# Sampling matrices split first and turned by the DMA engines instead of TensorE, in a fused attention and deformable-convolution kernel

## The chip, the core and the metric

The kernel is one program on one core of a Trainium2 chip. Its instructions run on five engines with a queue each: TensorE (PE, matmuls), VectorE (DVE), ScalarE (ACT), GpSimd (POOL) and SyncE (SP, which here only issues DMAs). Engines wait for each other by semaphores. The metric is the device time of one execution in microseconds, lower is better, as the median over runs.

## The reference

The input is `x`, 32 images of 192 channels and 32 x 32 pixels in float32. Two blocks follow, each behind a group normalization (32 groups) and each added to its input:

```python
x = x + attention(_gn(x))          # attention between channels, 1x1 projections
x = x + deform_block(_gn(x))

# attention, N = 1024 pixels
q, k, v = split(w_qkv @ x)                         # each 192 x N
attn = softmax(einsum('bcn,bdn->bcd', q, k) * 48 ** -0.5)
out = w_out @ (attn @ v) + b_out

# deformable 3x3 convolution
offset = clip(conv(x, off_w, off_b), -8, 8)        # 18 maps
mask = 2 * sigmoid(conv(x, mask_w, mask_b))        # 9 maps
# tap k of pixel (i, j) reads x, bilinearly, at (i - 1 + ky + dy, j - 1 + kx + dx), times the mask
y = einsum('bckhw,ock->bohw', p, proj_w) + proj_b
yn = (y - mean) * rsqrt(var + 1e-5) * gamma + beta # mean and variance over all images
return gelu(yn)
```

## The kernel before

The convolution samples after projecting. For each tap k, `z` is the projection of `x` with that tap's 192 x 192 weights, and the bilinear sampling is a matrix S_k of hat functions: the entry for output pixel p and source pixel (r, c) is mask x hat(y_p - r) x hat(x_p - c). So y = sum over k of S_k z_k. An image is cut into 8 tiles of 128 output pixels (4 rows). For a tile and one of the three rows of taps ky, the near sources are 8 rows of pixels, two chunks of 128. If an offset reaches further, a separate `far_pass` runs at the end of the image; a flag decides, and in this data the near branch is taken.

The names:
- A *step* is a tile and a ky: 24 per image. A *unit* is a step and one of its two source chunks: 48 per image (`UNITS`).
- `ay` and `bx` hold the row and column hats. They are made from `off`, the clipped offsets, by a subtraction (for `bx` on POOL, `column_distance`, line 1328; for `ay` on DVE, line 1122) and two activations on ACT (`column_hats`, lines 853 and 855; lines 844 and 846).
- `sT` is S transposed, output pixels on the partitions, 3 taps x 256 source pixels in float32. POOL makes one per step (line 1346), in a ring of 3.
- TensorE turns it (`turn_s`, line 653): three float32 transposes of 128 x 128 per unit, into one of two PSUM banks `sps`.
- Each turned unit is split in two float16 parts, high and rest: ACT casts to `sh` (line 896), DVE subtracts to `sl` (line 1157); a ring of 3.
- `convolve` multiplies (lines 670 to 672): three taps x (sh zh, sh zl, sl zh), nine matmuls of 192 columns into `acc`. After six units a tile is full; ACT copies it to `ypm`, TensorE turns it to `yt`, and DVE scales it to `ych` (`scale_y`, line 1219).
- `z` is made by `z_group` (lines 639 to 643), five matmuls of 288 columns per unit into one of two PSUM banks `zps`, ten units ahead (`AHEAD`), and split likewise by ACT (line 862) and DVE (line 1151). `z_group` of a unit waits for the `z` split of two units before.

The order is written out by hand. For each image `part1` walks over the 48 units on each engine, and `part0(u, b + 1, ...)`, the whole attention block, second normalization and offset convolution of the next image, is cut into 48 numbered pieces that are put behind the unit of the same number. Pieces that the prediction speaks of, by number: 0 to 4 statistics of the input; 6 to 10 first normalization on ACT and its residues on DVE (line 1014); 12 to 22 attention; 23 to 26 the sum `x1` and its statistics; 30 to 33 second normalization on ACT; 32 to 36 its residues and the moves of its planes to shifted copies on DVE (lines 1014 and 1020 to 1024); 38 and 39 the offset convolution on PE; 40 `off` (line 1118); 41 to 46 the hats. The DMAs on SyncE are few: `attended` stores `x1` and loads the input of the image after the next, `convolved` stores `y`. Batch statistics need all images, so a last pass reads `y` and `x1` again, applies the GELU and stores the output (from about 3805 us on).

## Time and profile before

| | |
|---|---|
| median of 3 runs | 4033.15 us (4030.4 to 4049.43) |
| the profiled execution | 4041.7 us, its span 4039.9 us, mean granted TensorE clock 0.966 |
| busy, share of the span | PE 88%, DVE 66%, ACT 52%, POOL 35% |
| DMA | 170.89 MB in all, mean 42 GB/s |

Time is busy time by the profiler; matmuls overlap in the record, so that a busy PE is not PE at its peak. A wait is idle time of an engine just before an instruction, named by what released it.

### The profile page before, as it was taken

To read this page: it belongs to the slowest core of one execution; us is meant where nothing else is said; L and a number is where in the kernel's file an instruction comes from. 1 tells how busy PE (TensorE), PEld (TensorE's weight loads), DVE (VectorE), ACT (ScalarE), POOL (GpSimd) and SP (SyncE) were. 2 spreads that over 40 slices of the span, in tenths; PEclk is the share of its full clock that TensorE was granted. 3 is DMA by queue.
4 is the path that set the end of the run, shared out by engine and by line. 5 is a ranking of instruction groups with operands and counts; after the bars stand their busy time and mean duration, and the time that the engine had idled before them with its cause. 6 is when DMAs were issued, how large, how long until landed. Compare 5 with 4: busy or idle time off the path is not lost.

```text
span 4039.9 us, 109164 instructions
## 1 busy us (share of the span) xinstructions
PE 3554.5 (88%) x38338; PEld 3036.9 (75%) x38338; DVE 2650.4 (66%) x5834; ACT 2108.1 (52%) x4790; POOL 1412.7 (35%) x1165
## 2 busy tenths in 40 slices
PE   3999999999999999999999999999999999999600
PEld 2788878888887878888887878788788888877600
DVE  3666776676777666666776676677666766776522
ACT  1555555555555555555555555555555555554422
POOL 1333333333333333434333333333333433333311
PEclk8999999999999999999999999999999999999855
DMA  2000000000000000000010000000000000000398
GB/s 63 20 11 28 28 28 20 28 28 28 10 28 28 20 28 28 28 17 21 29 28 21 28 28 28 10 28 28 28 20 28 28 24 14 28 28 10 96 370 299
DMA packets 50796, 170.89 MB, mean 42 GB/s; under 512 B 9664, under 2 KB 10880, under 8 KB 50176
## 3 DMA queue, kind: packets, MB, share of 16 engines
q1 hardware_dynamic: 39584, 136.75, 11.2%
q0 software_dynamic: 7168, 25.17, 1.6%
q8 instruction: 365, 5.98, 0.6%
q14 instruction: 255, 2.09, 0.2%
q10 hardware_dynamic: 3424, 0.90, 0.1%
HBM read 87.29 MB, written 75.50 MB: 40 GB/s over the span
## 4 chain that ended last, share of the span: by engine, by line
PE 65%; DVE 13%; issue 9%; DMA 4%; POOL 4%; ACT 3%; DVEq 1%; SPq 1%; ACTq 0%; POOLq 0%
PE sps L653 10%; PE acc L672 6%; PE acc L670 6%; PE acc L671 6%; PE l L581 4%; PE zps L639 3%; PE zps L643 3%; PE zps L641 3%; PE zps L640 3%; PE zps L642 3%; DVE zl L1151 3%; POOL sT L1346 3%; DMA xn<-x_scratch 2%; DVE sl L1157 2%; PE l L513 2%
## 5 line engine op out<-in xcount | busy, mean ns | idle before, releaser
L1346 POOL TENSOR_TENSOR sT<-ay,bx 128x768 f32<-128x768 f32 x768 | 1149.3, 1507 | 1394.6 <-PE sps L653 1326.2
L1157 DVE TENSOR_TENSOR sl<-sps,sh 128x384 f16<-128x384 f32 x1536 | 847.8, 552 | 560.7 <-ACT sh L896 555.9
L672 PE MATMUL acc<-zh,sl 128*128 128x192 f16 x4608 | 1134.6, 246 | 22.4 <-issue 22.4
L670 PE MATMUL acc<-zh,sh 128*128 128x192 f16 x4608 | 1134.6, 246 | 0.3 <-ACT ypm L923 0.3
L671 PE MATMUL acc<-zl,sh 128*128 128x192 f16 x4608 | 1134.5, 246 | 0.0
L896 ACT CAST sh<-sps 128x384 f16<-128x384 f32 x1536 | 741.4, 483 | 705.3 <-PE sps L653 696.9
L862 ACT CAST zh<-zps 128x288 f16<-128x288 f32 x1536 | 620.2, 404 | 668.4 <-PE zps L643 643.7
L1151 DVE TENSOR_TENSOR zl<-zps,zh 128x288 f16<-128x288 f32 x1536 | 694.2, 452 | 353.5 <-ACT zh L862 345.2
L653 PE MATMUL sps<-eye,sT 128*128 128x128 f32 x4608 | 786.3, 280 | 130.7 <-DVE sl L1157 96.6
L653 PEld LDWEIGHTS sps<-eye,sT 128*128 128x128 f32 x4608 | 531.7, 141 | 287.0 <-DVE sl L1157 158.0
L672 PEld LDWEIGHTS acc<-zh,sl 128*128 128x128 f16 x4608 | 451.3, 98 | 25.4 <-issue 25.3
L671 PEld LDWEIGHTS acc<-zl,sh 128*128 128x128 f16 x4608 | 451.3, 98 | 17.2
L670 PEld LDWEIGHTS acc<-zh,sh 128*128 128x128 f16 x4608 | 451.1, 98 | 2.5 <-DVE sl L1157 0.5
L639 PE MATMUL zps<-wpr_h,x_hi_a 128*128 128x288 f16 x1344 | 385.0, 286 | 0.8 <-DVE zl L1151 0.3
L640 PE MATMUL zps<-wpr_l,x_hi_a 128*128 128x288 f16 x1344 | 384.9, 286 | 0.0
L642 PE MATMUL zps<-wpr_h,x_hilo_b 128*128 128x288 f16 x1344 | 384.9, 286 | 0.0
L643 PE MATMUL zps<-wpr_l,x_hilo_b 128*128 128x288 f16 x1344 | 384.9, 286 | 0.0
L641 PE MATMUL zps<-wpr_h,x_lo_a 128*128 128x288 f16 x1344 | 384.9, 286 | 0.0
L1328 POOL TENSOR_TENSOR bx<-off,cx_sb 128x576 f32<-128x576 f32 x128 | 155.6, 1216 | 459.2 <-DVE off L1118 459.2
L1310 POOL TENSOR_TENSOR rstd<-gvar,mhalf 128x2 f32<-128x2 f32 x64 | 44.9, 702 | 557.7 <-DVE gvar L1008 557.7
L581 PE MATMUL l<-wof,x2s_hi_a 128*128 128x54 f16 x1536 | 183.0, 186 | 9.8 <-DVE x2w_hilo_b L1024 9.8
L581 PE MATMUL l<-wof,x2s_lo_a 128*128 128x54 f16 x1536 | 182.8, 186 | 0.0
(200 smaller groups left out, 6488.8 us busy)
## 6 DMA issues: line engine op xcount, KB each, us to landing
xin<-in_x SPq DMA_DIRECT2D x32, 512.0 KB, 5.2
xin<-in_x SPq DMA_DIRECT2D x64, 256.0 KB, 5.7
x_scratch<-x SPq DMA_DIRECT2D x32, 512.0 KB, 2.8
y_scratch<-ych SPq DMA_DIRECT2D x32, 512.0 KB, 2.7
zh<-y_scratch SPq DMA_DIRECT2D x20, 512.0 KB, 11.6
zl<-x_scratch SPq DMA_DIRECT2D x20, 512.0 KB, 12.8
out<-zh POOLq DMA_DIRECT2D x20, 512.0 KB, 9.3
x_scratch<-x SPq DMA_DIRECT2D x32, 256.0 KB, 3.5
```

What stands on the lines that cost most here:

```text
L581: mm = pe.matmul(o, src[:, row * W:(row + ROWS_T) * W], wof[:, m, k].rearrange("p i j -> p (i j)"), start=(k == 0 and n == 0), stop=(k == ...
L639: pe.matmul(o, at(0), wpr_h[:, 0, ky, n], start=True, stop=False)
L640: pe.matmul(o, at(0), wpr_l[:, 0, ky, n], start=False, stop=False)
L653: mm = pe.transpose(sps[u % 2][:, kx * P:(kx + 1) * P], sT[:, g, kx, c * P:(c + 1) * P], eye32[:, :])
L670: pe.matmul(acc[:, 0:C], s_h, zh[:, j, ky, z], start=start and kx == 0, stop=False)
L671: pe.matmul(acc[:, 0:C], s_h, zl[:, j, ky, z], start=False, stop=False)
L672: mm = pe.matmul(acc[:, 0:C], s_l, zh[:, j, ky, z], start=False, stop=stop and kx == 2)
L862: act.copy(z_piece(zh, g, par), zps[:, g % 2, 0:KO // 2]).then_inc(z_hi, 1)
L896: act.copy(sh[:, u % S_RING].rearrange("p k n -> p (k n)"), sps[u % 2][:, 0:3 * P]).then_inc(s_hi, 1)
L1151: dve.tensor_tensor(z_piece(zl, g, par), zps[:, g % 2, 0:KO // 2], z_piece(zh, g, par), ALU.subtract)\
L1157: dve.tensor_tensor(one(sl), sps[u % 2][:, 0:3 * P], one(sh), ALU.subtract).then_inc(s_lo, 1)
L1346: pool.tensor_tensor(sT[:, p % ST_RING].rearrange("p k (r x) -> p k r x", r=R), a, x_, ALU.mult)\
```

## The change

`sT` stays as POOL makes it, but it is split before it is turned. Per step, ACT casts all 768 columns of `sT` to the high half of `sT_hl`, and DVE subtracts for the low half; both now read SBUF. SyncE then issues one transposing DMA (`dma_start_transpose`) that turns the twelve 128 x 128 blocks (high and low, three taps, two chunks) into `s_hl`, a ring of 4 slots with a completion semaphore each, and `convolve` waits for the slot instead of for `s_lo`. The splits run four steps ahead (`S_AHEAD`), and the next image's preparation is moved up by six units (`EARLY`), so that its last six pieces' places are taken by the first six of the image after. Since the hats are needed sooner than the old ones are free, `bx` becomes a ring of two quarter-images, and its later quarters are made at other places. The far pass gets tiles of its own.

```diff
-        bx = sb("bx", [P, 2, TILES * TAPS, W])
+        BX_RING = 2
+        bx = sb("bx", [P, BX_RING, 2 * TAPS, W])
...
-        S_RING = 3
-        sh = sb("sh", [P, S_RING, 3, P], F16)
-        sl = sb("sl", [P, S_RING, 3, P], F16)
+        S_RING = 4
+        sT_hl = sb("sT_hl", [P, S_RING, 2, 3 * R * W], F16)
+        s_hl = sb("s_hl", [P, S_RING, 2, 3, 2, P], F16)
+        f_sh = sb("f_sh", [P, 3, P], F16)
+        f_sl = sb("f_sl", [P, 3, P], F16)
...
-            part1(0, 0, True, FRONT)
+            part1(0, 0, 2, FRONT)
...
+        def prepare(part0, u, b, par, more):
+
+            if u + EARLY < UNITS:
+                if more:
+                    part0(u + EARLY, b + 1, 1 - par)
+            elif more == 2:
+                part0(u + EARLY - UNITS, b + 2, par)
+
+        def prepare_second(part0):
+            for u in range(EARLY):
+                part0(u, 1, 1)
...
+        STEPS = 3 * TILES
+        S_AHEAD = 4
+        EARLY = 6
+
+        def s_step(u):
+
+            if u >= UNITS - S_AHEAD:
+                return u - (UNITS - S_AHEAD), True
+            if u % 2 == 0 and u // 2 + S_AHEAD < STEPS:
+                return u // 2 + S_AHEAD, False
+            return None, False
+
+        def turned(p, b):
+
+            return 16 * (STEPS // S_RING) * b + 16 * (p // S_RING) + 16
...
+            def turn_s(p, b):
+                if p >= S_RING or not first(b):
+                    sp.wait_ge(sz_done, UNITS * b + 2 * (p - S_RING) + 2)
+                    sp.sem_inc(turn_free, 1)
+                sp.wait_ge(s_lo, STEPS * b + p + 1)
+                sp.sem_inc(turn_begun, 1)
+                slot = p % S_RING
+                sp.dma_start_transpose(s_hl[:, slot].rearrange("p h k c n -> p (h k c) n"),
+                                       sT_hl[:, slot].rearrange("p h n -> p (h n)")).then_inc(s_turned[slot], 16)
+
+            def image(b, more, edge=None):
+                for p in range(STEPS):
+                    turn_s(p, b)
+                    if p == 8 and not first(b):
+                        convolved(b - 1)
...
+                    if p == 15 and more:
+                        attended(b + 1, more == 2)
...
-            def turn_s(u, b):
-                t, ky, c = u // 6, u % 6 // 2, u % 2
-                if c == 0:
-                    pe.wait_ge(st_made, 24 * b + 3 * t + ky + 1)
-                if u >= 2 or not first(b):
-                    pe.wait_ge(s_lo, UNITS * b + u - 1)
-                g = (3 * t + ky) % ST_RING
-                for kx in range(3):
-                    mm = pe.transpose(sps[u % 2][:, kx * P:(kx + 1) * P], sT[:, g, kx, c * P:(c + 1) * P], eye32[:, :])
-                mm.then_inc(s_ps, 1)
-
             def convolve(u, b, par):
                 i, ky, c = u // 6, u % 6 // 2, u % 2
-                pe.wait_ge(s_lo, UNITS * b + u + 1)
+                if c == 0:
+                    pe.wait_ge(s_turned[u // 2 % S_RING], turned(u // 2, b))
...
-                    if more:
-                        part0(u, b + 1, 1 - par)
+                    prepare(part0, u, b, par, more)
...
-            def split_s(u, b):
-                act.wait_ge(s_ps, UNITS * b + u + 1)
-                if u >= S_RING or not first(b):
-                    act.wait_ge(sz_done, UNITS * b + u - S_RING + 1)
-                act.copy(sh[:, u % S_RING].rearrange("p k n -> p (k n)"), sps[u % 2][:, 0:3 * P]).then_inc(s_hi, 1)
+            def split_s(p, b):
+                act.wait_ge(st_made, STEPS * b + p + 1)
+                if p >= S_RING or not first(b):
+                    act.wait_ge(s_turned[p % S_RING], turned(p - S_RING, b))
+                act.copy(sT_hl[:, p % S_RING, 0], sT[:, p % ST_RING].rearrange("p k n -> p (k n)")).then_inc(s_hi, 1)
...
-                    if u % 12 == 4 and u < 36:
-                        column_hats(u // 12 + 1, b, par)
+                    if u in (3, 13, 25):
+                        column_hats((3, 13, 25).index(u) + 1, b)
...
-            def split_s(u, b):
-                dve.wait_ge(s_hi, UNITS * b + u + 1)
-                one = lambda t: t[:, u % S_RING].rearrange("p k n -> p (k n)")
-                dve.tensor_tensor(one(sl), sps[u % 2][:, 0:3 * P], one(sh), ALU.subtract).then_inc(s_lo, 1)
+            def split_s(p, b):
+                dve.wait_ge(s_hi, STEPS * b + p + 1)
+                dve.tensor_tensor(sT_hl[:, p % S_RING, 1], sT[:, p % ST_RING].rearrange("p k n -> p (k n)"),
+                                  sT_hl[:, p % S_RING, 0], ALU.subtract).then_inc(s_lo, 1)
...
+                if q >= BX_RING or not first(b):
+                    pool.wait_ge(st_made, STEPS * b + 6 * (q - BX_RING) + 6)
...
                     if p >= ST_RING or not first(b):
-                        pool.wait_ge(s_ps, UNITS * b + 2 * (p - ST_RING) + 2)
+                        pool.wait_ge(s_lo, STEPS * b + p - ST_RING + 1)
...
-                    if p in (1, 4, 10):
-                        column_distance((1, 4, 10).index(p) + 1, b, par)
+                    if p in (1, 6, 12):
+                        column_distance((1, 6, 12).index(p) + 1, b, par)
                     if more:
-
-                        for u in (2 * p - 4, 2 * p - 3):
-                            part0(u, b + 1, 1 - par)
+                        for u in range(2):
+                            part0(2 * (p - S_AHEAD) + EARLY + u, b + 1, 1 - par)
```

The order on VectorE around the moves, before (in the first image; `sl` and `zl` are the two splits, `x_hilo_b` a residue, `x2s` and `x2w` the shifted planes and seams):

```order
L1151 TENSOR_TENSOR zl<-zps,zh 128x288
L1014 TENSOR_TENSOR x_lo_a<-xn,x_hi_a 128x1024
L1157 TENSOR_TENSOR sl<-sps,sh 128x384
L1151 TENSOR_TENSOR zl<-zps,zh 128x288
L1020 COPY x2s_hi_a<-x_hi_a 128x32x31
L1021 COPY x2s_hi_a<-x_hi_a 128x32x31
L1023 COPY x2w_hi_a<-x_hi_a 128x96
L1024 COPY x2w_hi_a<-x_hi_a 128x96
L1157 TENSOR_TENSOR sl<-sps,sh 128x384
L1151 TENSOR_TENSOR zl<-zps,zh 128x288
L1014 TENSOR_TENSOR x_hilo_b<-xn,x_hilo_b 64x1024
L1157 TENSOR_TENSOR sl<-sps,sh 128x384
```

The same place after (`sT_hl` is the new split of `sT`):

```order
L1185 TENSOR_TENSOR zl<-zps,zh 128x288
L1048 TENSOR_TENSOR x_lo_a<-xn,x_hi_a 128x1024
L1185 TENSOR_TENSOR zl<-zps,zh 128x288
L1054 COPY x2s_hi_a<-x_hi_a 128x32x31
L1055 COPY x2s_hi_a<-x_hi_a 128x32x31
L1057 COPY x2w_hi_a<-x_hi_a 128x96
L1058 COPY x2w_hi_a<-x_hi_a 128x96
L1190 TENSOR_TENSOR sT_hl<-sT,sT_hl 128x768
L1185 TENSOR_TENSOR zl<-zps,zh 128x288
L1048 TENSOR_TENSOR x_hilo_b<-xn,x_hilo_b 64x1024
L1185 TENSOR_TENSOR zl<-zps,zh 128x288
L1054 COPY x2s_lo_a<-x_lo_a 128x32x31
```

What moved: every preparation piece is still followed by one `zl` split, but the `sl` split of each unit has become one wider split of `sT` in every second unit.

The order on GpSimd at the turn from one image to the next, before; the row of line 1328 is the next image's first column distance, which waits for `off`:

```order
L1346 TENSOR_TENSOR sT<-ay,bx 128x768
L1326 REGISTER_ALU
L1328 TENSOR_TENSOR bx<-off,cx_sb 128x576
L1342 ISA
L1346 TENSOR_TENSOR sT<-ay,bx 128x768
L1338 ISA
L1340 ISA
L1342 ISA
L1346 TENSOR_TENSOR sT<-ay,bx 128x768
```

After (line 1373 is the column distance, 1392 makes `sT`, the three ISA rows in a run carry waits for the hats):

```order
L1392 TENSOR_TENSOR sT<-ay,bx 128x768
L1369 REGISTER_ALU
L1371 ISA
L1373 TENSOR_TENSOR bx<-off,cx_sb 128x576
L1387 ISA
L1392 TENSOR_TENSOR sT<-ay,bx 128x768
L1387 ISA
L1392 TENSOR_TENSOR sT<-ay,bx 128x768
L1383 ISA
L1385 ISA
L1387 ISA
L1392 TENSOR_TENSOR sT<-ay,bx 128x768
```

What moved: the column distance stands one `sT` tile earlier; two tiles of the old image follow it where one did, and then the waits and the new image's first tile.

The order on SyncE in the loop, before: the stores of `y` and `x1` follow each other directly.

```order
L415 ISA
L415 DMA xin<-in_x 64x1024
L434 ISA
L434 DMA y_scratch<-ych 128x1024
L435 ISA
L435 DMA y_scratch<-ych 64x1024
L426 ISA
L427 ISA
L427 DMA x_scratch<-x 128x1024
L428 ISA
```

After, around the ninth step of an image:

```order
L475 DMA_TRANSPOSE s_hl<-sT_hl 128x12x128
L470 ISA
L472 ISA
L475 DMA_TRANSPOSE s_hl<-sT_hl 128x12x128
L470 ISA
L472 ISA
L475 DMA_TRANSPOSE s_hl<-sT_hl 128x12x128
L465 ISA
L465 DMA y_scratch<-ych 128x1024
L466 ISA
L466 DMA y_scratch<-ych 64x1024
L470 ISA
```

What moved: each store of `y` now stands in a row of 24 transposing DMAs per image, each behind a wait for a free slot (line 472's ISA row) and one for the split.

## Rows read from the trace of the kernel before

**Rows 1.** The page: busy time and share by engine, and the chain that ended last.

```profile
PE 3554.5 (88%) x38338; PEld 3036.9 (75%) x38338; DVE 2650.4 (66%) x5834; ACT 2108.1 (52%) x4790; POOL 1412.7 (35%) x1165
...
PE 65%; DVE 13%; issue 9%; DMA 4%; POOL 4%; ACT 3%; DVEq 1%; SPq 1%; ACTq 0%; POOLq 0%
PE sps L653 10%; PE acc L672 6%; PE acc L670 6%; PE acc L671 6%; PE l L581 4%; PE zps L639 3%; PE zps L643 3%; PE zps L641 3%; PE zps L640 3%; PE zps L642 3%; DVE zl L1151 3%; POOL sT L1346 3%; DMA xn<-x_scratch 2%; DVE sl L1157 2%; PE l L513 2%
```

**Rows 2.** Windows: from:to, length, each engine's busy time, granted clock, DMA.

```profile
1512.80:1522.90 10.10, 9.32 (x92) 8.18 (x90) 9.35 (x21) 4.84 (x14) 4.46 (x4) 1.00 0.02 6
1522.90:1532.90 10.00, 9.98 (x96) 9.08 (x95) 7.51 (x21) 7.71 (x17) 6.01 (x7) 1.00 0.19 66
...
1590.60:1597.70 7.10, 6.97 (x72) 6.25 (x70) 6.05 (x13) 7.10 (x13) 4.01 (x4) 1.00 0.01 3
1597.70:1606.00 8.30, 5.85 (x53) 4.44 (x50) 8.24 (x18) 3.13 (x9) 2.87 (x2) 1.00 0.00 0
...
1615.30:1628.30 13.00, 12.28 (x122) 10.84 (x120) 9.67 (x26) 8.95 (x24) 7.97 (x6) 1.00 0.01 1
sum 115.50, PE 110.61 PEld 94.54 DVE 80.54 ACT 63.86 POOL 42.56; mean PE 11.06 PEld 9.45 DVE 8.05 ACT 6.39 POOL 4.26
```

**Rows 3.** The chain in a plain stretch: start, length, what.

```profile
1516.95 0.33 PE sps L653 x3
...
1518.02 0.12 PE zps L639
...
1518.63 0.33 PE sps L653 x3
```

**Rows 4.** Line 1118, the clipped offsets: durations, first and last start.

```profile
L1118 DVE TENSOR_SCALAR off<-off x32: 234/235/236, 104.8 to 3713.3; 128x144 f32<-128x144 f32 x32
```

**Rows 5.** Groups by line: shapes, count | busy us, mean ns | idle before.

```profile
L1157 DVE TENSOR_TENSOR sl<-sps,sh 128x384 f16<-128x384 f32 x1536 | 847.8, 552 | 560.7 <-ACT sh L896 555.9 <-issue 1.2
...
L896 ACT CAST sh<-sps 128x384 f16<-128x384 f32 x1536 | 741.4, 483 | 705.3 <-PE sps L653 696.9 <-PE acc L672 2.5
L1151 DVE TENSOR_TENSOR zl<-zps,zh 128x288 f16<-128x288 f32 x1536 | 694.2, 452 | 353.5 <-ACT zh L862 345.2
L862 ACT CAST zh<-zps 128x288 f16<-128x288 f32 x1536 | 620.2, 404 | 668.4 <-PE zps L643 643.7
...
L810 ACT COPY xt<-l 128x768 f16<-128x768 f16 x128 | 102.1, 799 | 13.8 <-PE l L525 13.8
```

**Rows 6.** Three lines: duration ns min/median/max, first and last start.

```profile
L1014 DVE TENSOR_TENSOR xl_a<-xn,xh_a x32: 1226/1710/1716, 46.3 to 3628.5; 128x1024 f16<-128x1024 f32 x32
...
L1023 DVE COPY x2w_hi_a<-x_hi_a x32: 175/1448/1451, 92.5 to 3692.8; 128x96 f16<-128x96 f16 x32
...
L1346 POOL TENSOR_TENSOR sT<-ay,bx x768: 1470/1482/1698, 108.2 to 3797.5; 128x768 f32<-128x768 f32 x192
```

**Rows 7.** Groups by line, ACT alone: normalization and hats.

```profile
L853 ACT ACTIVATE bx<-bx 128x576 f32<-128x576 f32 x128 | 88.5, 691 | 0.1
...
L795 ACT ACTIVATE xn<-x,nbias,rstd 128x1024 f32<-128x1024 f32 x64 | 80.5, 1258 | 14.0 <-POOL nbias L1314 14.0
```

**Rows 8.** Timeline at an image's turn: start, length, engine, line [idle before <-releaser].

```profile
1502.79 1.16 POOL L1328 TENSOR_TENSOR bx<-off,cx_sb 128x576 f32<-128x576 f32 x1 [14.28 <-DVE off L1118]
...
1506.27 0.31 PEld L653 LDWEIGHTS sps<-eye,sT 128*128 128x128 f32 x3 [0.92 <-DVE sl L1157]
```

**Rows 9.** DMA queues, and issues with KB each and median us to landing.

```profile
q1 hardware_dynamic: 39584, 136.75, 11.2%
...
q10 hardware_dynamic: 3424, 0.90, 0.1%
...
xin<-in_x SPq DMA_DIRECT2D x64, 256.0 KB, 5.7
x_scratch<-x SPq DMA_DIRECT2D x32, 512.0 KB, 2.8
```

**Rows 10.** SyncE's time for one issue: ns min/median/max.

```profile
L427 SPq DMA_DIRECT2D x_scratch<-x x32: 337/346/373, 83.3 to 3677.6; - x32
```

More of the change, by code:

```diff
@@ L218, in build @@
         st_made = sem("st_made")
-        s_ps = sem("s_ps")
+        s_turned = [sem(f"s_turned{i}") for i in range(S_RING)]
+        turn_free = sem("turn_free")
+        turn_begun = sem("turn_begun")
         s_hi = sem("s_hi")
@@ L312, in pairs_of_images @@
         @contextmanager
-        def pairs_of_images(eng, start, end):
+        def pairs_of_images(eng, start, end, step=2):
             name, only = f"images_{nc.next_id()}", [eng.engine]
@@ L320, in pairs_of_images @@
                 edge = []
-                yield nc.snap(count, min_val=start, max_val=end - 1), edge
-                nc.regs_alu(count, count, 2, op=ALU.add)
+                yield nc.snap(count, min_val=start, max_val=end - step), edge
+                nc.regs_alu(count, count, step, op=ALU.add)
                 eng.br_lt(count, end, on_true=f"{name}_loop", on_false=f"{name}_end").branch_hint(edge[0])
@@ L901, in part1 @@
                         split_z(g, b, par)
-                    split_s(0, b)
-                    split_s(1, b)
+                    for p in range(S_AHEAD):
+                        split_s(p, b)
+                    prepare_second(part0)
                 for u in units:
@@ L906, in part1 @@
                         edge.append(act.mark_branch_hint_location())
[L907 to L910 removed]
+                    p, of_next = s_step(u)
+                    if p is not None and not of_next:
+                        split_s(p, b)
+                    elif p is not None and more:
+                        split_s(p, b + 1)
                     if u == 24:
@@ L1236, in part1 @@
                         split_z(g, b, par)
-                    split_s(0, b)
-                    split_s(1, b)
+                    for p in range(S_AHEAD):
+                        split_s(p, b)
+                    prepare_second(part0)
                 for u in units:
```

108 lines of the change are left out of this document (53 added, 55 removed).

## The prediction

> **What bounds the kernel now.** First the page's busy shares and the chain that ended last [rows 1]: TensorE is busy 88% of 4039.9 us and holds 65% of the chain, with the transposes of `sT` (line 653) its largest line, 10%. Then one image of the steady loop cut into stretches [rows 2]; the reader should compare the columns stretch by stretch, since a share over the span hides what each stretch waits for. From 1597.7 us VectorE (DVE) is busy 8.24 of 8.30 us and TensorE (PE) only 5.85; from 1512.8 DVE has 9.35 of 10.10; over all ten stretches, 115.5 us, PE has 110.6, DVE 80.5, ScalarE (ACT) 63.9, GpSimd (POOL) 42.6. The granted clock is 1.00, the 2.4 GHz level. Then the chain inside a plain stretch [rows 3]: a unit (one of 48 per image) takes 1.68 us, from 1516.95 to 1518.63, of which the three transposes are 0.33, the nine products of lines 670 to 672 0.74 and the five `zps` products 0.61. So PE sets the pace, except where VectorE is full.
>
> Line 1118 runs once per image, at 104.8 us first and 3713.3 last [rows 4]: the mean image is 3608.5 / 31 = 116.4 us, and the one of rows 2 stands for all. My sums are against the profiled run, 4041.7 us. The median, 4033.15, is 8.5 lower; I subtract that at the end.
>
> **Removed from PE.** 4608 transposes, three per unit, 0.33 us per unit: 48 x 0.33 = 15.8 us per image, 507 us for 32, if PE set the pace everywhere. Image: 115.5 - 15.8 = 99.7. A plain unit would be 1.68 - 0.33 = 1.35 us, and a step (two units, one `sT` tile) 2.70.
>
> **Changed on ACT and DVE.** Per step ACT casts 2 x 483 ns and DVE subtracts 2 x 552 ns from PSUM, beside two `z` splits at 404 and 452 [rows 5]. Afterwards each has one operation of 768 columns from SBUF. For ACT the copy of line 810 has that width: 799 ns. For DVE, 288 columns at 452 and 384 at 552 give 1.04 ns a column, so 768 is 952 ns [rows 5]. ACT saves 0.17 and DVE 0.15 us a step, which leaves 80.5 - 3.7 = 76.8 us of DVE work per image, 77% of 99.7. What DVE costs is decided by where that work lies.
>
> **Given back where DVE is full.** The next image's preparation keeps its operations and moves up six units; the work on `y` stays. PE may run ahead of the `z` splits by two buffers: one unit and the nine products, 1.35 + 0.74, less cast and subtraction, 0.40 + 0.45, leave some 1.2 us; then PE stands.
> (a) Lines 1014 and 1020 to 1024, preparation units 32 to 36, now at 26 to 30. Today 15.4 us go by from 1590.6 to 1606.0 for seven units of 1.68, so 3.6 us of stall. Afterwards DVE needs in units 26 to 31: six `z` and half `s` splits at 0.92, 5.5; the residues 1.71 and, at the line's least, 1.22; moves of 2.46 + 2.46 + 1.2, whose largest part is a 96-column copy of 1.45 [rows 6]; `scale_y`, 1.07. Together 15.6 us. Units 24 and 25 add 1.8, and ACT holds DVE up there: two normalizations at 1.26, two hat operations at 0.69, two casts of `z` and one of `s` are 5.5 us [rows 5, 7], of whose 3.7 beyond DVE's own I count half. 1.8 + 1.9 + 15.6 - 1.2 = 18.1 us for eight units, where PE alone needs 10.8: 7.3 of stall against 3.6 now. Lost: 3.7 us per image.
> (b) Preparation units 41 to 47 and the next image's units 0 to 9. Three stretches of rows 2 (from 1615.3, 1512.8 and 1522.9) hold these 17 units in 33.1 us with DVE busy 26.5. Without transposes PE needs 27.5, and DVE 26.5 - 1.2 = 25.3, 92% of it, in pieces of up to 1.7 us, with the splits of steps 0 to 3 packed one per unit at 44 to 47. Two engines that wait for each other at such a load don't both fit: I take 12% of 27.5, 3.3 us.
>
> **Moved on POOL.** The column distance of the next image stood before step 23 and now stands before step 22. Today POOL runs it as soon as `off` is clipped, for 1.16 us, `sT` follows, and PE loses 0.92 us to the split behind it at 1506.27 [rows 8]. Afterwards `off` comes in unit 34, and ACT wants step 22 at unit 36, with its `z` cast queued behind that wait; PE feels it at unit 38. `off` 1.1 + distance 1.2 + `sT` 1.5 + cast 0.8 + subtraction 0.95 + a `z` split 0.45, 6.0 us, against the 4.5 to 6 us until unit 38's `z`: between 0 and 3 us with the lag of DVE, I take 1.5.
>
> **Added: 768 transposing DMAs**, each 128 x 1536 half floats, 393 KB, on SyncE's queue. This trace has none. Lower bound: queue q1 moves 136.75 MB in 11.2% of the 16 engines' 4039.9 us, 302 GB/s, so 1.3 us. The nearest row is q10's, whose 3424 packets have 263 bytes in the mean and took 0.1% of that time, 19 ns each; the transfer has 1536 source pieces of 256 bytes, 96 per engine: 1.8 us. Upper bound: if every 32-byte piece of the destination cost those 19 ns, 768 per engine are 14.6 us [rows 9]. I take 1.8, and for latency the stores of 512 KB, landed 2.8 us after issue, and 0.35 us of SyncE's time per issue [rows 9, 10]: some 3.5 us. The rate stands under the 2.70 of a step. The slot is free one step after its split begins, which leaves three steps, 8.1 us, even beside an input load of 5.7 us [rows 9]. So PE's work hides it, and if it takes longer than a step this cover is gone (rivals 1 and 4). Only step 0 of an image is tight, split at unit 44 and used at 48: 0.8 + 0.95 + 1.2 of lag + 3.5 = 6.5 against four units and the last `y` transposes, 5.8, and the statistics product: I put 0.3 us. Behind SyncE's new waits stand its stores and loads; their data is there by units 6 and 20, and they are issued behind steps 8 and 15, at units 10 and 24: nothing.
> By the Trainium skill (Advanced Engine Details and Errata, X-Bar Transpose (TRN2)) a transposing DMA reaches 350 to 400 GB/s; DMA: Bandwidth & Descriptors (Latency and other measured facts) has 261 with a non-contiguous middle dimension. By these it would be 1.0 to 1.5 us, an estimate that no run here shows yet.
>
> **The sum.** Per image 99.7 + 3.7 + 3.3 + 1.5 + 0.3 = 108.5, 7.0 less than 115.5. 31 x 7.0 = 217; the last image has no preparation and gains about 12; the start grows by about 5 (four steps and six preparation units ahead of the loop). 4041.7 - 224 = 3818, in terms of the median 3809. **Forecast 3810 us**, own range 3700 to 3920 (gains of 3.5 to 10.5 us per image).
>
> **Rivals.**
> 1. *The transposing DMA is too slow*, and SyncE's queue sets the pace. It decides from 115.5 / 24 = 4.8 us per step; 1.8 and 14.6 lie on both sides. At 5.5 us an image is 132 and the run 4033 + 32 x 16.5 = 4560; at 14.6 it would pass 11000. For it: no row shows a transpose, and the destination comes in 32-byte runs. Against: the source pieces have 256 bytes. 16%.
> 2. *DVE and POOL block each other.* The new subtraction reads two SBUF tensors, the old one PSUM and SBUF. Line 1014, with two SBUF inputs, takes at least 1226 ns but 1710 in the median, and the 96-column copy 175 against 1448, close to one POOL operation (1482) more [rows 6]. If each of 768 subtractions lost 0.48 us, 369, half of them where DVE is full, 185: 3995. At 1.27 each, 4300. Against: POOL's next `sT` is released by this subtraction itself and is over 1.5 us later, while the next subtraction comes at least 1.75 later. 12%, three quarters of it still faster.
> The Trainium skill (SBUF — State Buffer, SBUF: two separate sides) has this as an exclusive lock, held for the whole instruction by either a GpSimd operation or a DVE one with two SBUF inputs. Rows 6 agree.
> 3. *Nothing is given back*: 4033 - 507 = 3526, up to 3620 with part of (a). Against it stands DVE's 8.24 of 8.30 us [rows 2]. 8%.
> 4. *Transposes at 3.3 to 4.6 us*: at 3.9 some six plain steps an image lose 1.2 us each, less the slack 3 to 5: 3810 + 32 x 4 = 3940. 5%, two fifths of it no change.
>
> **Chances.** Forecast 59%, rivals 16, 12, 8, 5. Faster by over 0.5% (what a measurement of this kernel can tell from no change): 59 + 9 + 8 + 3 = 79%. Within 0.5%: 2 + 2 = 4%. Slower: 16 + 1 = 17%. The range 3580 to 4040 leaves out rival 1 and half of rival 3.
>
> **What would show it.** Right: transposes landing in under 5 us, PE idle for `z` splits only and mostly beside line 1014 and the copies, plain units of 1.35 us, images of 105 to 112 us, a subtraction of about 0.95 us. Wrong: PE waiting for a transposed slot throughout the image (rivals 1, 4), a subtraction of over 1.3 us in the median (rival 2), or units of 1.35 us even beside the moves (rival 3).

## The result and the profile after

| | before | after |
|---|---|---|
| median | 4032.94 us (4030.4 to 4049.43, 4 runs) | **4277.0 us** (4273.95 to 4278.61, 4 runs) |
| ratio, 95% interval | | **1.0595 [1.0566, 1.0624]**, slower |
| span of the profiled run | 4039.9 us | 4276.9 us |
| granted TensorE clock, mean | 0.966 | 0.897 |

The page of the kernel after, where it answers to [rows 1] and [rows 9]; the last two rows are two of its DMA rows.

```profile
PE 3346.2 (78%) x33730; PEld 2667.4 (62%) x33730; DVE 2659.5 (62%) x5066; ACT 2010.7 (47%) x4022; POOL 1517.8 (35%) x1165
...
PEclk8899989999999999899899998899998999999855
...
q1 hardware_dynamic: 1243808, 438.83, 54.2%
...
s_hl<-sT_hl SPq DMA_TRANSPOSE x768, 3.7
```

TensorE has less to do and is busy a smaller share of a longer run. The clock row has 8s all through the loop; the kernel before has 9s there. (The chain of waits covers only 8% of this run's span, so I read waits and windows instead.) The first and last start of the clipped offsets, against [rows 4]:

```profile
L1152 DVE TENSOR_SCALAR off<-off x32: 234/234/236, 106.0 to 3946.9; 128x144 f32<-128x144 f32 x32
```

(3946.9 - 106.0) / 31 = 123.9 us per image, where it was 116.4 and 108.5 was forecast. Two windows of about one image (columns as in [rows 2]):

```profile
1604.00:1616.00 12.00, 7.65 (x58) 5.66 (x57) 8.77 (x20) 4.04 (x10) 6.14 (x6) 0.91 0.82 119
...
1672.00:1696.00 24.00, 18.10 (x154) 14.63 (x152) 16.78 (x32) 14.09 (x26) 9.84 (x9) 0.93 0.75 160
```

TensorE is busy 64 and 75% in them, VectorE 73 and 70%. And the clock is under 1.00, which no window of [rows 2] was. Such long windows hide what each wait looks like, so here are shorter ones of the same image around four of TensorE's waits: units 5, 15, 28 to 32, and 38:

```profile
1622.40:1626.40 4.00, 1.68 (x16) 1.07 (x13) 1.55 (x3) 3.63 (x8) 3.11 (x3) 1.00 0.53 98
1649.10:1655.00 5.90, 3.54 (x25) 2.15 (x23) 3.74 (x7) 1.03 (x3) 2.59 (x2) 0.99 0.58 108
1684.10:1700.20 16.10, 10.57 (x181) 8.57 (x179) 15.00 (x27) 8.01 (x15) 4.59 (x4) 1.00 0.72 120
1709.90:1715.60 5.70, 2.92 (x20) 2.26 (x19) 3.68 (x9) 4.36 (x9) 3.57 (x3) 0.77 0.24 45
```

They differ. In the third, around the moves, VectorE is busy 15.00 of 16.10 us; in the first ScalarE is, 3.63 of 4.00; in the second and fourth no engine is near full. TensorE's waits, in all, times, longest, after:

```profile
PE zps L688 <- DVE zl L1185: 332.6, 312, 5.4
PE l L553 <- DVE mv L1032: 95.4, 64, 14.2
PE l L561 <- DVE gram L1105: 75.7, 32, 2.8
PE acc L710 <- ACT ypm L958: 55.8, 39, 1.7
...
PE acc L710 <- DMA s_hl<-sT_hl: 0.6, 1, 0.6
```

and before:

```profile
PE sps L653 <- DVE sl L1157: 96.6, 125, 1.2
...
PE l L512 <- DVE gram L1071: 21.5, 32, 2.8
...
PE l L504 <- DVE mv L998: 16.9, 2, 14.2
```

The transposing DMAs are waited for once, 0.6 us. What TensorE waits for is VectorE's `z` split, the statistics and the Gram matrix. What such a wait leaves behind shows around the Gram matrix, in windows of 2 us and in the timeline:

```profile
1647.00:1649.00 2.00, 2.00 (x22) 1.83 (x21) 0.46 (x1) 1.49 (x6) 2.00 (x3) 1.00 0.38 71
...
1651.00:1653.00 2.00, 0.03 (x1) 0.03 (x1) 1.92 (x7) 0.05 (x1) 1.48 (x1) 1.00 0.37 70
1653.00:1655.00 2.00, 2.00 (x9) 0.99 (x10) 0.29 (x1) 0.00 (x0) 0.00 (x0) 0.98 0.69 127
1655.00:1657.00 2.00, 2.00 (x13) 1.74 (x13) 0.65 (x1) 1.26 (x3) 0.00 (x0) 0.50 0.00 0
1657.00:1659.00 2.00, 2.00 (x9) 1.16 (x8) 0.77 (x2) 0.40 (x1) 1.48 (x1) 0.67 0.00 0
```

```profile
1611.98 0.25 PE L712 MATMUL acc<-zh,s_hl 128*128 128x192 f16 x1
1612.06 0.25 PE L710 MATMUL acc<-zh,s_hl 128*128 128x192 f16 x1
...
1652.97 0.59 PE L561 MATMUL l<-wo,gram 128*128 128x192 f32 x2 [2.36 <-DVE gram L1105]
...
1655.25 0.37 PE L712 MATMUL acc<-zh,s_hl 128*128 128x192 f16 x1
1655.41 0.37 PE L710 MATMUL acc<-zh,s_hl 128*128 128x192 f16 x1
```

TensorE stands 2.36 us, works on, and then has the granted clock 0.50, the 1.2 GHz level: the same matmuls start 0.16 us apart instead of 0.08. A wait can be paid a second time, in slow columns behind it.

**Where the time went.** A mean clock c over a span is 2 x (1 - c) of it at half rate: 2 x 0.103 x 4276.9 = 881 us after, 2 x 0.034 x 4039.9 = 275 before. 606 us more, which cost half of that, 303 us. The spans differ by 237 = -507 (transposes removed) + 303 (clock) + 441, and this rest is what TensorE waits more. By its matmul records, as a mean of images 2 to 29:

| per image, us | period | no matmul under way | at 1.2 GHz |
|---|---|---|---|
| before | 116.3 | 5.6 | 0.1 |
| after | 124.2 | 19.5 | 19.9 |

116.3 - 15.8 + (19.5 - 5.6) + (19.9 - 0.1) / 2 = 124.3. Below, *gaps* and *half clock* are the two last columns. The rule that time at the low clock costs half of itself is also in the Trainium skill (TensorE: Matmul & The Clock Gate, Terms); this sum agrees with it.

### The profile page after: what moved, and what is told of

It is laid out like the page before. It is cut to its first block and busy times, and to the rows that moved or that the text cites. A ratio compares the mean times of both kernels' runs of the same rounds, so it can differ in the third digit from the quotient of the medians.

```text
span 4276.9 us, 97266 instructions
## 1 busy us (share of the span) xinstructions
PE 3346.2 (78%) x33730; PEld 2667.4 (62%) x33730; DVE 2659.5 (62%) x5066; ACT 2010.7 (47%) x4022; POOL 1517.8 (35%) x1165
## 5 line engine op out<-in xcount | busy, mean ns | idle before, releaser
L1392 POOL TENSOR_TENSOR sT<-ay,bx 128x768 f32<-128x768 f32 x768 | 1235.2, 1622 | 1304.0 <-ACT bx L888 685.8
L1190 DVE TENSOR_TENSOR sT_hl<-sT,sT_hl 128x768 f16<-128x768 f32 x768 | 877.2, 1142 | 656.8 <-ACT sT_hl L929 656.1
L710 PE MATMUL acc<-zh,s_hl 128*128 128x192 f16 x4608 | 1190.3, 258 | 84.5 <-ACT ypm L958 55.8
L711 PE MATMUL acc<-zl,s_hl 128*128 128x192 f16 x4608 | 1189.1, 258 | 27.3 <-issue 27.3
L712 PE MATMUL acc<-zh,s_hl 128*128 128x192 f16 x4608 | 1188.7, 258 | 0.0
L929 ACT CAST sT_hl<-sT 128x768 f16<-128x768 f32 x768 | 638.8, 832 | 264.7 <-POOL sT L1392 167.3
L688 PE MATMUL zps<-wpr_h,x_hi_a 128*128 128x288 f16 x1344 | 410.3, 305 | 287.2 <-DVE zl L1185 284.5
L710 PEld LDWEIGHTS acc<-zh,s_hl 128*128 128x128 f16 x4608 | 471.7, 102 | 210.0 <-issue 89.4
L711 PEld LDWEIGHTS acc<-zl,s_hl 128*128 128x128 f16 x4608 | 472.8, 103 | 73.0 <-issue 29.9
L712 PEld LDWEIGHTS acc<-zh,s_hl 128*128 128x128 f16 x4608 | 474.9, 103 | 6.4 <-issue 1.3
L688 PEld LDWEIGHTS zps<-wpr_h,x_hi_a 128*128 128x128 f16 x1344 | 137.1, 102 | 364.3 <-DVE zl L1185 356.1
L957 ACT COPY ypm<-acc 128x192 f32<-128x192 f32 x256 | 81.9, 320 | 325.1 <-PE acc L712 324.6
```

Source lines behind the costliest of these rows:

```text
L688: pe.matmul(o, at(0), wpr_h[:, 0, ky, n], start=True, stop=False)
L710: pe.matmul(acc[:, 0:C], s_h, zh[:, j, ky, z], start=start and kx == 0, stop=False)
L711: pe.matmul(acc[:, 0:C], s_h, zl[:, j, ky, z], start=False, stop=False)
L712: mm = pe.matmul(acc[:, 0:C], s_l, zh[:, j, ky, z], start=False, stop=stop and kx == 2)
L929: act.copy(sT_hl[:, p % S_RING, 0], sT[:, p % ST_RING].rearrange("p k n -> p (k n)")).then_inc(s_hi, 1)
L1190: dve.tensor_tensor(sT_hl[:, p % S_RING, 1], sT[:, p % ST_RING].rearrange("p k n -> p (k n)"), sT_hl[:, p % S_RING, 0], ALU.subtract).then ...
```

## The experiments

All times stand against the kernel before on the same chip, 4028 to 4034 us. Each run has the gaps and half clock of one image.

| run | median us | ratio to before, 95% | gaps | half clock |
|---|---|---|---|---|
| e1 hats early | 4107.75 | 1.0188 [1.0155, 1.022] | 17.1 | 13.2 |
| e2 distance later | 4251.4 | 1.0563 [1.0517, 1.0609] | 21.1 | 13.3 |
| e3 no transposing DMA | 4212.05 | 1.0438 [1.0401, 1.0476] | 19.4 | 15.8 |
| e4 before, a third of the transposes | 3939.23 | 0.9779 [0.9744, 0.9814] | 10.4 | 4.6 |
| e5 = e1 + e2 | 4090.66 | 1.0146 [1.0109, 1.0184] | 18.0 | 9.7 |
| e6 e1, two units ahead, not six | 4380.45 | 1.0866 [1.0834, 1.0899] | 22.6 | 20.2 |
| e7 after + fillers | 4143.36 | 1.027 [1.0239, 1.0302] | 9.5 | 0.1 |
| e8 e5, `z` split first | 4301.83 | 1.067 [1.063, 1.0709] | 20.4 | 21.6 |
| e9 e5 + fillers | 4045.01 | 1.0023 [1.0009, 1.0037] | 10.7 | 0.6 |
| e10 no moves | 4204.97 | 1.041 [1.0373, 1.0447] | 18.8 | 16.9 |
| e11 four `z` banks | 4332.89 | 1.0752 [1.0717, 1.0786] | 20.6 | 25.9 |
| e12 e5, four `z` banks | 4189.53 | 1.0397 [1.0359, 1.0435] | 18.6 | 19.3 |
| e13 e5, 3 `z` banks, 2 accumulators | 4192.35 | 1.0404 [1.0376, 1.0432] | 18.3 | 20.6 |
| e14 e9, 2 accumulators, row distance early | 4093.7 | 1.0169 [1.015, 1.0189] | 12.0 | 2.7 |
| e15 e13, row distance early | 4135.0 | 1.0275 [1.0257, 1.0294] | 19.1 | 14.8 |
| e16 a third of VectorE's split | 4090.49 | 1.0134 [1.0103, 1.0165] | 17.1 | 11.7 |
| e17 a third of ScalarE's | 4232.39 | 1.0492 [1.0467, 1.0518] | 19.6 | 16.2 |
| e18 both | 4051.43 | 1.0042 [1.0029, 1.0055] | 16.5 | 10.6 |

(With fillers the gaps are what the fillers leave open.)

**Are the DMAs the cost?** e3 leaves all 768 out; TensorE multiplies by the unturned `sT_hl`, in a ring of 8.

```diff
-                turn_s(p, b)
-                    pe.wait_ge(s_turned[u // 2 % S_RING], turned(u // 2, b))
+                    pe.wait_ge(s_lo, STEPS * b + u // 2 + 1)
```

> The changed kernel without its 768 transposing DMAs: TensorE multiplies with the split sT as it lies, not turned (the transposition is left out), in a ring of eight. All else is equal, the wait for a slot included. Theory 1: within 1% of the changed kernel, 4240 to 4290, since the DMAs land in 3.7 us and hide. Theory 2: well faster, under 4150.

65 us less, gaps as they were; the 4.1 us per image less at half clock make some 62 of it. That is outside what either theory expected, but the other 180 us over the kernel before remain: the DMAs aren't the main cause.

**The order of the hats and the column distance.** e1 puts quarter 1 into the previous image and moves quarters 2 and 3 on ScalarE; e2 puts the next image's column distance behind the last step on GpSimd; e5 does both; e6 is e1 with `EARLY = 2`.

```diff
-                    if u in (3, 13, 25):
-                        column_hats((3, 13, 25).index(u) + 1, b)
+                    if u in (5, 14):
+                        column_hats((5, 14).index(u) + 2, b)
+                    if u == 42 and more:
+                        column_hats(1, b + 1)
```

```diff
-                            part0(2 * (p - S_AHEAD) + EARLY + u, b + 1, 1 - par)
+                            k = 2 * (p - S_AHEAD) + EARLY + u
+                            if k != 41:
+                                part0(k, b + 1, 1 - par)
+                        if p == STEPS - 1:
+                            column_distance(0, b + 1, 1 - par)
```

> The changed kernel, with the later column hats made earlier on ACT: quarter 1 at unit 42 of the image before (was unit 3), quarter 2 at 5 (was 13), quarter 3 at 14 (was 25). Theory 1 (the loss is in waits behind the two-quarter ring of bx and the early column distance, plus the half clock that follows idle stretches of TensorE): POOL's 686 us of waiting for the hats nearly goes, the gaps of TensorE in units 6, 7 and 28 (1.7 + 0.5 + 1.9 us an image) go and with them some 2 of the 20 us at half clock: 4 to 5 us an image, so 4277 - 145 = about 4130. Theory 2 (the transposing DMAs themselves cost the time): no change, 4260 to 4290. Theory 3 (the lock between DVE and POOL, which the wider subtraction meets): no change or a little slower.

> The changed kernel, with the next image's first column distance on POOL behind step 23 instead of before step 22. Theory 1: the gap of 2.8 us in unit 38 goes and the 2.8 us at half clock in units 38 to 40 with it: 3.5 to 4 us an image, about 4155. If the next image's step 0 now comes late instead, a gap opens at units 44 to 48 and the gain is under 1 us an image. Theories 2 and 3: no change.

> The hats made earlier (4108) and the column distance behind step 23 (4251 against 4277) together. If the two are independent: 4108 - 26 = 4080. If POOL, no longer late, profits more from the second: down to 4050.

> The version with earlier hats, with the preparation of the next image moved up by two units (EARLY = 2) instead of six. Theory that the move itself does harm (heavy pieces of preparation now fall together with y_stats and scale_y): 4040 to 4090. If the six units only shift the same waits to other places: 4090 to 4130. If the splits of the next image's first steps now come too late: above 4130, with gaps in units 44 to 2.

e1 gains the most of these changes of order: 169 us, more than its theory expected. The `sT` group of the kernel after and GpSimd's first wait in e1 (the second number group is idle time and its releaser):

```profile
L1392 POOL TENSOR_TENSOR sT<-ay,bx 128x768 f32<-128x768 f32 x768 | 1235.2, 1622 | 1304.0 <-ACT bx L888 685.8
```

```profile
POOL sT L1395 <- DVE sT_hl L1193: 1126.0, 371, 6.8
```

With the ring of two quarters GpSimd stood 685.8 us for ScalarE's hats; in e1 that wait is no longer among its first. But gaps fell by only 2.4 us per image; more than half of the gain, 3.4 us per image, is half clock. e2 moved its gap instead of removing it: unit 38 stands 1.9 us instead of 2.8, unit 32 1.8 instead of 0.7, and over the image the gaps grew by 1.6 us. Its 26 us come from the half clock. With e1 it adds 17 us, which the intervals of e1 and e5 don't tell from nothing. e6 is 273 us slower than e1, the third of its expectations, with 5.8 us of gaps in units 44 to 2: of the two distances, six units ahead is much the better.

**Is the clock a cause of its own?** e7 adds 165 matmuls per image whose product nothing reads, in front of the places where TensorE waits; e9 adds 114 to e5 (its expectation says 112).

```diff
+            def fill(n):
+                for _ in range(n):
+                    pe.matmul(sps[0][:, 0:C], eye16[:, :], wpr_h[:, 0, 0, 0:C], start=True, stop=True)
...
+                    fill({0: 8, 6: 18}.get(u, 0))
                     convolve(u, b, par)
```

> The changed kernel with 165 matmuls of 192 columns a image that compute nothing used, put on TensorE just before the waits of units 0, 1, 6, 15, 22, 26, 28, 29, 31, 38 and 46, with a little less length than the gaps there (8 to 30 each, 0.08 us apiece, some 13 us an image). Theory that idle stretches drop the granted clock and that this costs half of the 19.9 us an image at half clock: the time at half clock falls under 10 us an image and the run to 4090 to 4160. If the clock is only a symptom of waits that bound the run anyway: 4270 to 4330.

> The kernel of e5 (hats of the next image early, column distance behind step 23) with 112 matmuls per image added whose product nothing reads, put where TensorE still waits in e5: ahead of the waits of units 0, 5, 6, 26, 28, 29, 31, 38 and of the Gram and statistics steps. Theory A (the gaps cost twice, once as waiting and once as columns at 1.2 GHz behind them): the time at half clock falls from 9.65 us per image to near 0, gaps stay at about 18 us or shrink to the part that the fillers don't cover; 4090.7 less 0.5 x 9.65 x 30 = 145 gives about 3945, and up to 4000 where fillers delay a step that was already due. That would be 1 to 2% under the kernel before, the first version here to beat it. Rival (e7's gain came only from the long stretches that the hats left, which e5 has filled already): 4060 to 4100, no change against e5.

The clock row of e7's page, and TensorE's busy time:

```profile
PE 3531.0 (85%) x39010; PEld 2925.1 (71%) x39010; DVE 2645.5 (64%) x5066; ACT 2002.1 (48%) x4022; POOL 1517.6 (37%) x1165
...
PEclk8999999999999999999999999999999999999855
```

5280 instructions more than the kernel after, and 134 us less: the clock is back at 9s. Since these matmuls do no useful work, the clock is shown to be a cause of its own. Of the 303 us it was priced at less than half came back: 165 x 0.08 = 13.2 us of fillers per image took the place of only 10.0 us of gaps. e9 expected 3945 to 4000 and gave 4045: the half clock went (9.7 to 0.6), yet of the 145 us it was priced at 46 came; here 114 x 0.08 = 9.1 us of fillers replaced 7.3 us of gaps. It is the fastest version here that leaves no work out, and it isn't faster than before: 1.0023 [1.0009, 1.0037].

**Was the old order's slack the same?** e4 is the kernel before with one transpose per unit instead of three; the other two thirds of each turned tile stay stale.

```diff
-                for kx in range(3):
+                for kx in range(3 if u < 2 and first(b) else 1):
```

> The kernel before, with one of the three transposes per unit instead of three (two thirds of each sampling matrix are left as they were). 2/3 of 15.8 us of TensorE's time go per image. If TensorE's time is worth its full price in the old order: 4033 - 338 = 3695. My prediction's step (a fifth to a half is given back where VectorE is full): 3750 to 3850. If idle stretches bring the half clock here too, over 3900.

At 0.33 us per unit 338 us of transposes were left out; 89 us came back against the kernel before on the same chip, so the expectation with the half clock (over 3900) held. By its matmul records TensorE's own time fell by 9.1 us per image and the period by 2.1. So even without a changed order, DMA or ring, about three quarters of what TensorE saves turns into gaps (5.6 to 10.4 us per image) and half clock (0.1 to 4.6).

**Is VectorE full where term (a) has it, and does the order of splits matter?** e10 leaves out nearly all of the moves from the third image on; e8 puts the `z` split ahead of the `sT` split on ScalarE and VectorE in every unit of e5.

> The changed kernel without nearly all of the copies that move the second normalization's result into the shifted planes (left out from the third image on, so those planes keep stale values and the output is not the reference's). It tests the prediction's term (a), 3.7 us per image given back in units 24 to 31 because the vector engine is full there. If the vector engine's own work binds there: gaps in units 26 to 33 shrink by about 4 us per image, with the columns at half clock behind them some 1.5 us less; 4277 less 30 x (4 + 0.75) = about 4135, 4090 to 4180. Rival (the waits there come from the order of ScalarE and GpSimd, not from the amount of vector work): 4260 to 4290.

> Both moves of e5, and in every unit ACT and DVE now split z before they split sT. TensorE waits for z two units on, for the steps four on. If waits behind the step split are what delays z (the z cast stands behind it on ACT): gaps shrink by 2 to 4 us an image against e5, 60 to 150 us less. If the sum of VectorE's work binds: within 20 us of e5.

e10 lies between its two expectations, and it took away less than it was priced for: VectorE's busy time falls by 72.6 us in all (2659.5 to 2586.9), 2.4 us per image, since the residues of (a) stayed and the copies are short here. Units 24 to 33 take 26.8 us instead of 28.6, and their gaps fall from 6.2 to 5.2 us. The run is 72 us shorter. So the work on VectorE does count around the moves, as (a) had it and as its 15.00 of 16.10 us say. That 72 us came for 72.6 is partly chance: over the image the gaps fell by 0.7 us and the half clock by 3.0. e8 went the wrong way; that earlier `z` splits make `sT` and all behind it later is my reading, which no run tests.

**Too few buffers, or too slow partners?** TensorE may be only two `z` products ahead. The banks of `sps` are free, so e11 and e12 give them to `z`; e13 gives one to a second accumulator; e15 also makes the row distance one unit earlier; e14 is e9 with the second accumulator and the earlier row distance, and two `z` banks.

```diff
+        def z_at(g):
+            return (zps[:, 0], zps[:, 1], sps[0], sps[1])[g % 4][:, 0:KO // 2]
-                if g >= 2 or not first(b):
-                    pe.wait_ge(z_lo, UNITS * b + g - 1)
+                if g >= 4 or not first(b):
+                    pe.wait_ge(z_lo, UNITS * b + g - 3)
```

```diff
-                if u % 6 == 0 and (i > 0 or not first(b)):
-                    pe.wait_ge(y_pm, TILES * b + i)
+                if u % 6 == 0 and (i > 1 or not first(b)):
+                    pe.wait_ge(y_pm, TILES * b + i - 1)
...
+ ... s_product(..., (acc, sps[1])[i % 2])
```

> The changed kernel with four PSUM banks for the five products of z instead of two: the two banks of sps, which the change left without a use in the main loop, join the ring, and TensorE waits for the z split of four units back instead of two. No instruction is added or taken away. Theory A (most of TensorE's gaps come from how far it may run ahead of ScalarE and VectorE: each burst of preparation work there holds a z split up for more than the one or two units that TensorE has in hand, while the mean load of both leaves room): the gaps fall from 19.5 to 8 to 13 us per image and the columns at half clock from 20 to 5 to 12 us; 4277 less 30 x (9 + 5) gives about 3860, 3780 to 3980. Theory B (VectorE and ScalarE are full over whole stretches, so TensorE meets the same wait a few units later): gaps fall by less than 3 us per image, 4150 to 4280. The prediction's terms (a) and (b) are B's kind.

> The same four banks together with e5's two moves (hats of the next image early, column distance behind step 23). Theory A: from e5's 4090.7, gaps 18.0 to 8 to 12 us per image and half clock 9.7 to 2 to 6 us: about 4091 - 30 x (8 + 3) = 3760, 3700 to 3880, well under the kernel before (4030). Theory B: 4000 to 4090.

> e5 with the two free PSUM banks given out differently than in e12: three banks for the products of z, and two accumulators in turn, so that TensorE may begin the next tile before ScalarE has copied the last one. Theory A (coupling, latency): with both rings deeper the gaps fall from e5's 18 us per image to 8 to 12 and half clock to under 6: 3780 to 3930. Theory B (the work and the mutual waits of ScalarE, VectorE and GpSimd take as long as an image does now; more buffers only move TensorE's gaps to the steps that need a result of theirs at once, the Gram matrix, the statistics and the offset convolution): gaps stay at 16 to 19, fewer and longer, 4070 to 4200.

> e9 (e5 with 112 matmuls per image that nothing reads) with two accumulators in turn, and the row distance of the second half of the tiles one unit earlier on VectorE, right in reach of the first. z keeps its two banks. Theory A: the wait for the accumulator's copy and ScalarE's 3 us wait for the distance go, some 3 us per image in all, from 4045 to about 3950. Theory B: 4020 to 4060, as e9.

> e13 with the row distance of the second half of the tiles one unit earlier on VectorE, so that ScalarE, seen to wait 3.0 us for it in front of its copies, finds it ready. If such waits between ScalarE and VectorE are what paces the image: 2 to 3 us per image less gap than e13 and some half clock with it, 60 to 120 us less than e13. If the wait only moves: within 20 us of e13.

TensorE's waits in e12 and then in e13:

```profile
PE acc L713 <- ACT ypm L964: 261.5, 95, 4.6
PE l L633 <- DVE x2w_hilo_b L1064: 123.7, 32, 9.8
PE l L556 <- DVE mv L1038: 107.9, 64, 14.2
...
PE zps L691 <- DVE zl L1191: 4.2, 1, 4.2
```

```profile
PE l L556 <- DVE mv L1039: 151.7, 64, 14.2
PE zps L691 <- DVE zl L1192: 131.0, 174, 4.8
PE l L633 <- DVE x2w_hilo_b L1065: 112.7, 32, 9.8
PE l L577 <- DVE xhl_b L1055: 93.4, 32, 9.5
```

My theory A fell in all five, and only e13 came out where theory B expected it: e11, e12 and e14 are slower than either theory. The wait for `z` splits goes from 332.6 to 4.2 us in e11 and from 286.0 to 4.2 in e12, and comes back at the accumulator (55.8 to 325.5, and 43.7 to 261.5); with two accumulators it comes back at the statistics, the offset convolution and the first normalization, which need a result at once. Without fillers the sum stays at 18 to 21 us per image. The same sum now comes in fewer, longer waits: gaps of 1.5 us or more hold 17.9 us per image in e11, 11.8 in the kernel after. And more columns run at 1.2 GHz (19.9 to 25.9 us in e11): deeper buffers made it slower. e14 is 49 us slower than e9, with more gaps (10.7 to 12.0) and more half clock (0.6 to 2.7); why the second accumulator costs there, no run shows. One such wait in e12 (last bracket: idle before, releaser):

```profile
2055.04 0.26 PE L713 MATMUL acc<-zh,s_hl 128*128 128x192 f16 x1 [3.29 <-ACT ypm L964]
```

```profile
2053.41 0.44 ACT L880 ACTIVATE ay<-ay 128x288 f32<-128x288 f32 x1 [3.03 <-DVE ay L1162]
...
2054.76 0.23 ACT L964 COPY ypm<-acc 128x64 f32<-128x64 f32 x1
```

```profile
2049.81 1.92 DVE L1196 TENSOR_TENSOR sT_hl<-sT,sT_hl 128x768 f16<-128x768 f32 x1 [0.28 <-ACT sT_hl L932]
2051.65 0.44 DVE L1191 TENSOR_TENSOR zl<-zps,zh 128x288 f16<-128x288 f32 x1
2052.02 0.68 DVE L1277 BATCH_NORM_STATS2 ystats<-ych 128x512 f32 x1
2052.62 0.76 DVE L1162 TENSOR_TENSOR ay<-off,cy_sb 128x288 f32<-128x288 f32 x1
```

```profile
2049.80:2053.40 3.60, 1.95 (x19) 1.47 (x17) 3.59 (x5) 0.58 (x2) 3.60 (x3) 1.00 0.61 114
```

TensorE waits for ScalarE's copy, which stands in ScalarE's queue behind an activation that waits 3.03 us for VectorE's distance, which stands behind an `sT` split of 1.92 us, twice the 958 ns of its median in the kernel after. In this stretch VectorE and GpSimd are both busy throughout (3.59 and 3.60 of 3.60 us), and ScalarE and TensorE stand in line behind them. e15 moved that distance one unit forward: 57 us less than e13, all of it half clock (20.6 to 14.8 us per image); the gaps grew by 0.8.

**Whose work?** e16, e17 and e18 cut the `sT` split to 256 of 768 columns on VectorE, ScalarE and both, from the second image on (the rest of the low half, high half or both stays stale).

```diff
+                n = 3 * R * W if first(b) else R * W
-                dve.tensor_tensor(sT_hl[:, p % S_RING, 1], ...
+                dve.tensor_tensor(sT_hl[:, p % S_RING, 1, 0:n], ...
```

> The changed kernel with VectorE's subtraction in the sT split done on 256 of its 768 columns from the second image on (the other columns of the low part stay stale). By VectorE's rate the operation goes from 958 to some 420 ns: 24 x 0.54 = 13 us less VectorE work per image, and the same time off the way from GpSimd's sT to the transposing DMA. Theory C (VectorE's work is what TensorE's gaps come from, as terms (a) and (b) have it): gaps fall from 19.5 to 10 to 13 us per image, half clock from 20 to about 10: 4277 - 30 x (8 + 5) = 3890, 3830 to 3980. Theory D (the waits are a chain through ScalarE, VectorE and GpSimd in turn, in which any operation counts by its length only where it is on the chain): gaps fall by 3 to 5 us, 4080 to 4180.

> The same for ScalarE: its cast in the sT split on 256 of 768 columns from the second image on (the rest of the high part stale), 834 to some 370 ns, 24 x 0.46 = 11 us less ScalarE work per image. VectorE's work is as before. Theory C: little, gaps down by under 2 us per image, 4180 to 4280, since ScalarE is busy only 47% of the time. Theory D: gaps fall by 3 to 5 us, as in e16, 4080 to 4180.

> Both cuts together. Theory C: about e16 (within 40 us of it). Theory D: about the sum of the two gains, 3900 to 4050. If neither engine's amount of work matters: 4200 to 4280.

The group in e16 and in e17 (busy us, mean ns):

```profile
L1191 DVE TENSOR_TENSOR sT_hl<-sT,sT_hl 128x256 f16<-128x256 f32 (+1 forms) x768 | 442.3, 576 | 646.2 <-ACT sT_hl L929 644.9
```

```profile
L930 ACT CAST sT_hl<-sT 128x256 f16<-128x256 f32 (+1 forms) x768 | 321.0, 418 | 279.0 <-POOL sT L1394 167.8
```

VectorE lost 24 x (1142 - 576) = 13.6 us of work per image; gaps fell by 2.5 and half clock by 8.2. ScalarE lost 24 x (832 - 418) = 9.9 us; gaps didn't fall, half clock fell by 3.7. Both together: gaps down by 3.0. So VectorE counts and ScalarE hardly does, but neither C (gaps to 10 to 13) nor D (3 to 5 each) holds: under a fifth of the work taken from VectorE comes back as gap. With the half clock it is nearly half, 6.3 us of the period, and e16's 187 us are the most that a single edit brought back. e16 doesn't tell VectorE's work from what its operation holds up on GpSimd: a tile of `sT` takes 1553 ns there in the mean, 1622 in the kernel after.

## Why the prediction was wrong

**The step that failed first is the unit of the sum: a stall was priced at its own length.** "7.3 of stall against 3.6 now" and "I take 12% of 27.5, 3.3 us" were added at 2.4 GHz, because every window of [rows 2] has clock 1.00. There is no term for the clock behind a stall. It measured 19.9 us at 1.2 GHz per image, 9.9 us of time, 303 us over the run, more than the whole forecast gain of 224. Taken off the 4277, that gives about 3975, an estimate: faster than before and inside the range of 3580 to 4040, but outside the 3700 to 3920 that the forecast gave itself. No run reached it; e7, which takes the half clock away with fillers, gave 4143.

**The second is the size of the stalls**, 8.8 us per image forecast, 13.9 measured. The two together, 9.9 and 5.1, are what lies between the forecast 7.0 us less per image and the measured 7.9 more:

| term | forecast | gaps, after less the same pieces before |
|---|---|---|
| (a) around the moves, now units 24 to 33 | +3.7 | 6.2 - 2.6 = +3.6 |
| column distance, unit 38 | +1.5 | 2.8 - 0.6 = +2.2 |
| (b) and step 0, units 39 to 47 and 0 to 7 | +3.6 | 7.3 - 0.8 = +6.5 |
| units 16 to 23, Gram matrix and statistics | 0 | 3.3 - 1.4 = +1.9 |

(The other units lost 0.3 us of gap.) (a) has the right size and the right reason, VectorE full around the moves, 15.00 of 16.10 us; but not the right parts. The moves take 2.6 us instead of 6.1, and the two residues 4.6 instead of 2.9: that these errors cancel in part is luck. (b) missed the hats: I read the ring of two quarters in the diff and didn't price ScalarE's in-order wait and GpSimd's behind it (e1: 169 us with the clock). The Gram wait is there before, 21.5 us in all, and 75.7 after: my reading, which no run tests, is that TensorE now comes to it earlier. I looked mainly for places where VectorE is full; the waits of units 5, 15 and 38, some 7.5 of the 19.5 us, stand where it is busy 1.55 of 4.00, 3.74 of 5.90 and 3.68 of 5.70 us.

**What was right.** The table gives forecast, measured, and the row.

| | forecast | measured |
|---|---|---|
| plain unit | 1.35 us | 1.36 us |
| ACT cast, 768 columns | 799 ns | 832 ns |
| DVE subtraction, median | 952 ns | 958 ns |
| transposing DMA, landing | 3.5 us | 3.7 us |
| the same, rate | 1.8 us | 2.4 us |

```profile
1618.63 0.29 PE L688 MATMUL zps<-wpr_h,x_hi_a 128*128 128x288 f16 x1
1619.99 0.29 PE L688 MATMUL zps<-wpr_h,x_hi_a 128*128 128x288 f16 x1
```

```profile
L1190 DVE TENSOR_TENSOR sT_hl<-sT,sT_hl x768: 936/958/2239, 120.8 to 4030.2; 128x768 f16<-128x768 f32 x192
...
L929 ACT CAST sT_hl<-sT 128x768 f16<-128x768 f32 x768 | 638.8, 832 | 264.7 <-POOL sT L1392 167.3
```

The rate: q1 took 0.542 x 4276.9 = 2318 us of the 16 engines, before 0.112 x 4039.9 = 452; 1866 / 768 = 2.4 us for 393 KB, 162 GB/s. The Trainium skill has 350 to 400 GB/s (Advanced Engine Details and Errata, X-Bar Transpose (TRN2)) and 261 GB/s with a non-contiguous middle dimension (DMA: Bandwidth & Descriptors, Latency and other measured facts); neither is reached here.

**The rivals.** 1 and 4 (transposes too slow) didn't happen. 2 (VectorE and GpSimd block each other) happened at its mechanism, not at its size: the subtraction's mean is 1142 against the median 958, 768 x 0.18 = 141 us in all where it had 369; and a tile of `sT` on GpSimd takes 1622 ns in the mean, before 1507. 3 (nothing given back) missed on the other side. No rival had the outcome, slower with every transfer hidden; the chance of slower, 17%, was nearly all rival 1's.

**What stays open.** Why the gaps stay at 16 to 23 us, whatever is moved or buffered, is shown only by where they go, not derived. e16 and e10 say that VectorE's work takes part. Not run: less work on GpSimd, e16's cut together with e1's order, and the new order with the transposes still on TensorE, which would part the order from the rest.

## What to carry to other kernels

Before taking work from the engine that paces the loop, ask what its partners' queues look like when it comes earlier to every meeting: taking out part of it first (e4, one line) would have given the answer, about a quarter of the saving, without building the change. Price a stall of TensorE with the slow columns that can follow it (here 13.9 us more of stalls per image brought 9.9 us on top), and look at the granted clock in windows of 2 us, not only over the span. Look at the partners in windows of a few microseconds too: over the image VectorE is busy under 70% of the time, around the moves 93%. More buffers didn't shorten waits for partners in line here; they gathered them into longer ones, and those cost more clock.
